# A selective scan beside a decoded FFN: the scan's drive through ScalarE and TensorE transposes, two steps in each turn

## The reference

```python
# FFN of layer 0, h is the normalised x, wg, wu, wd are decoded from control points
out = (silu(h @ wg.T) * (h @ wu.T)) @ wd.T
# scan of layer 1, for each batch: channel d of 512, state n of 16, time l of 512
# delta = softplus(...), u = silu(conv(context @ in_proj))
state[d, n, l] = exp(delta[d, l] * A[d, n]) * state[d, n, l - 1] + delta[d, l] * u[d, l] * B[n, l]
y[d, l]        = sum over n of state[d, n, l] * C[n, l]  + D[d] * u[d, l]
```

## Time and profile before

| what | us |
|---|---|
| median of three runs (1612.72 to 1623.57) | 1617.37 |
| the profiled execution: device time | 1603.47 |
| its span | 1601.7 |
| PE, DVE, ACT, POOL busy in the span | 1322.5, 1092.9, 839.4, 1049.8 |
| stage B, from its first DMA to the last add | 182 to 855 |

### The profile page before, as it was taken

The page is one execution under the profiler, slowest core; times in us unless marked ns, Lnnn a source line. Parts: engine busy times, 40 slices in busy tenths (PEclk is TensorE's granted clock), DMA queues, the critical chain, the costliest instruction groups (busy, mean ns, idle before and its releaser), DMA issues. The chain is left out here.

```text
span 1601.7 us, 24508 instructions
## 1 busy us (share of the span) xinstructions
PE 1322.5 (83%) x5493; PEld 881.7 (55%) x5494; DVE 1092.9 (68%) x1961; ACT 839.4 (52%) x1363; POOL 1049.8 (66%) x656
## 2 busy tenths in 40 slices
PE   7999768987867776675765846999999999999997
PEld 3444323333423332332323435888888988888886
DVE  5777666666867687776777796666656666566554
ACT  6777634446645555564544673454444444454442
...
GB/s 298 119 104 76 185 125 124 137 118 191 173 196 178 221 181 191 179 217 190 179 181 238 267 35 103 202 204 193 200 188 191 207 196 200 198 200 199 197 142 121
DMA packets 108664, 282.09 MB, mean 176 GB/s; under 512 B 17329, under 2 KB 23138, under 8 KB 97474
## 3 DMA queue, kind: packets, MB, share of 16 engines
...
## 5 line engine op out<-in xcount | busy, mean ns | idle before, releaser
L857 PE MATMUL bank<-B_Wd,B_inter 128*128 128x512 f32 x512 | 282.7, 704 | 134.0 <-DVE X L1045 119.6
L1166 POOL TENSOR_TENSOR B_E<-B_dtu,B_BC 128x512 f32<-128x512 f32 (+3 forms) x121 | 312.4, 2734 | 15.7 <-DMA B_BC<-bc_d 15.7
L946 ACT ACTIVATE bank<-B_dtv,negA 128x512 f32<-128x512 f32 x256 | 175.2, 690 | 231.6 <-DVE B_E L1059 120.7
L2087 POOL DMA_INDIRECT out_x<-D_y,D_rows x144 | 234.1, 1626 | 82.6 <-issue 50.2
L1172 POOL TENSOR_TENSOR B_E<-B_E,B_BC 128x1536 f32<-128x1536 f32 x64 | 240.2, 3753 | 71.7 <-DVE B_E L1059 68.0
L857 PEld LDWEIGHTS bank<-B_Wd,B_inter 128*128 128x128 f32 x512 | 110.0, 225 | 306.5 <-issue 291.0
L1059 DVE TENSOR_TENSOR_SCAN B_E<-bank,B_E 128x512 f32<-128x512 f32 x192 | 227.5, 1210 | 32.0 <-ACT bank L946 17.6
L2052 POOL DMA_INDIRECT D_rows<-rows_d,D_source x144 | 153.7, 1067 | 125.8 <-DMA out_x<-D_y,D_rows 63.0
L1913 ACT ACTIVATE D_xT_hi<-bank 128x512 fp32r<-128x512 f32 x147 | 88.0, 599 | 230.1 <-PE bank L1822 229.6
L1833 PE MATMUL bank<-W_gu_hi,D_xT_hi 128*128 x584 | 200.8, 344 | 8.4 <-ACT D_xT_hi L1913 8.4
L1834 PE MATMUL bank<-W_gu_lo,D_xT_hi 128*128 x584 | 198.1, 339 | 0.0
...
...
## 6 DMA issues: line engine op xcount, KB each, us to landing
...
B_BC<-bc_d SPq DMA_DIRECT2D x128, 256.0 KB, 6.2
...
```

Source lines behind the costliest of these rows:

```text
L857: mm = pe.matmul(ps[:, :], chunk(4 * quarter + i)[:, t * P:(t + 1) * P], Wd[:, (4 * quarter + i) % NCH, :], start=i == 0, stop=i == 3)
L946: act.activation(dA[m % 2][:, :], dtv[:, c, :], ACT.Exp, scale=negA[:, c, n:n + 1]).then_inc(dA_done, 1)
L1166: g.tensor_tensor(E[:, s % NR, c:end, :], dtu[:, at:at + end - c, :], spread(BC[op % NBC][:, :], end - c), ALU.mult).then_inc(dbu_done, 1)
L2087: g.indirect_dma_start(a["out"], bass.IndirectOffsetOnAxis(ap=rows[i][:, ROW - 1:ROW].bitcast(U32), axis=0), ysb[:, i, :], None, compute_o ...
```

## The change

- The drive no longer comes from GpSimd. Stage A transposes `dtu` (four chunks of four 128x128 turns in each batch, TensorE into banks, ScalarE out of them) and stores it with time on partitions (`dtuT_d`); the rows B are transposed too and stay in SBUF (`BT`). In stage B ScalarE's `scale(s, t)` multiplies 128 time steps by B as a per-partition scalar into one of six buffers `scaled`, and TensorE's `drive(s, c)` turns four 128x128 blocks into one of two banks, where the scan reads them.
- The decays are written into `E`, in which the scan then writes its state in place; they wait for the gather of four steps before.
- GpSimd weighs all four chunks in two halves, `weigh_last` is gone, and only rows C are loaded (ring of two).
- The order of every engine in stage B is new: TensorE takes a `drive` and one part of the turn by turns, `down` is cut in halves and alternates between two banks, ScalarE prepares a whole step ahead of its scan in two parts, VectorE runs the eight scans of a turn with the rest between them. Turns have two steps (turns 7 and 15 one), and two steps remain after turn 31, beside the last four `down`. The statistics for later norms move from turns 1 and 2 to turns 9 and 10, one unit moves from turn 4 to turn 5, and some buffers are shared.

```diff
-TURN_UNITS += [[("gate_up", 5)] + [("down", k) for k in range(12, NCH)], [("gate_up", 6)], [("gate_up", 7)]]
+TURN_UNITS += [[("gate_up", 5)] + [("down", k) for k in range(12, NCH - 1)], [("gate_up", 6), ("down", NCH - 1)], [("gate_up", 7)]]
...
 ROW = D + NE + 1
...
+            def turn_dtu(b, c, ps):
+                for t in range(LT):
+                    mm = pe.transpose(ps[:, t * P:(t + 1) * P], dtu[:, c, t * P:(t + 1) * P], ident[:, :])
+                mm.then_inc(xT_ps, 1)
...
+                    if b:
+                        if e == 0:
+                            pe.wait_ge(dtu_done, b)
+                        if e == 2:
+                            pe.wait_ge(xT_sb, b * 9 - 3)
+                        else:
+                            pe.wait_ge(x1_done, b * 4 - 4 + (1, 2, 0, 4)[e])
+                        turn_dtu(b - 1, e, bank[DTU_BANK[e]])
+                        if e == 1:
+                            pe.wait_ge(x1_done, b * 4 - 1)
+                            turn_inputs(b - 1, bank[BT_BANK])
...
+            pe.wait_ge(c_sb, NB * 3)
+            pe.wait_ge(dtu_done, NB)
+            for c in range(KC):
+                turn_dtu(NB - 1, c, bank[2 + c])
+                if c == 1:
...
+
+            def dtu_turned(b, c, ps):
+                act.wait_ge(xT_ps, b * 9 + 5 + c + (c > 1))
+                act.activation(dtuT[:, :, c * P:(c + 1) * P], ps[:, :].rearrange("p (t d) -> p t d", t=LT), ACT.Copy).then_inc(xT_sb, 1)
...
+                    if b:
+                        dtu_turned(b - 1, e, bank[DTU_BANK[e]])
...
+                    for c in range(2):
+                        dtu_turned(b, c, bank[2 + c])
                     root_kept()
+                    for c in range(2, KC):
+                        dtu_turned(b, c, bank[2 + c])
...
-                    g.wait_ge(stored, b * 64)
+                    g.wait_ge(xT_ps, b * 9)
...
+            def load_row(s):
+                if s >= NC:
+                    sp.wait_ge(prod_done, 2 * (s - NC) + 2)
+                sp.dma_start(C_row[s % NC][:, :], bc_d[s // NS, NS + s % NS:NS + s % NS + 1, :].broadcast_to([P, L])).then_inc(ld_c[s % NC], 16)
...
+            for s in range(NC, STEPS):
                 b, n = s // NS, s % NS
-                if drives and n == NS - 1 and b < NB - 1:
...
+                load_row(s)
+                if b < NB - 1:
+                    if n == 8:
+                        load_dtu(b + 1, 0)
...
-            def down(n, ps):
+            def down(n, ps, half):
...
+                if half == 0:
...
+                    pe.wait_ge(used, chunk_job(2 * quarter + 1, 1) + 1)
+                    if n >= 2:
                         pe.wait_ge(add_done, n - 1)
...
+                    if n % 2 and n < 4 * (TURNS // 2 - 1):
+                        pe.wait_ge(f_lo, min(2 * quarter + 2 + t // 2 + 2, TURNS))
...
+                for i in range(2 * half, 2 * half + 2):
                     mm = pe.matmul(ps[:, :], chunk(4 * quarter + i)[:, t * P:(t + 1) * P], Wd[:, (4 * quarter + i) % NCH, :], start=i == 0, stop=i == 3)
-                mm.then_inc(y_ps, 1)
+                if half:
+                    mm.then_inc(y_ps, 1)
...
+            def drive(s, c):
+                m = KC * s + c
+                if m >= 2:
+                    pe.wait_ge(s_done, m - 1)
+                for t in range(LT):
+                    if c == 0:
+                        pe.wait_ge(scaled_done, LT * s + t + 1)
+                    mm = pe.transpose(drive_bank[m % 2][:, t * P:(t + 1) * P], scaled[:, (LT * s + t) % NSC, c * P:(c + 1) * P], ident[:, :])
+                mm.then_inc(drive_ps, 1)
...
-                gate_up(jj, 0)
-                gate_up(jj, 1)
-                sums = sums_at(jj)
-                if jj % NG == NG - 1 and jj < TURNS - 1:
-                    for t in range(LT):
-                        turn(LT * (jj // NG + 1) + t)
-                    pe.wait_ge(hT_done, LT * (jj // NG + 2))
-                    down(sums[0], Y_bank)
-                    features(jj + 1)
-                    down(sums[1], Y_bank)
-                else:
-                    if jj < TURNS - 1:
-                        features(jj + 1)
-                    for m in turn_units(jj):
-                        weights(m)
-                    for n in sums:
-                        down(n, Y_bank)
-            for t in range(LT):
-                down(2 * TURNS - 4 + t, T_bank[t % 2])
+                sums, units, steps = sums_at(jj), turn_units(jj), slots(jj)
+                PARTS = 8 + len(units)
+                for i, (s, c) in enumerate(steps):
+                    drive(s, c)
+                    for k in range(PARTS):
+                        if k * len(steps) // PARTS != i:
+                            continue
+                        if k < 2:
+                            gate_up(jj, k)
+                        if k == 2 and not last_of_batch(jj) and jj < TURNS - 1:
+                            features(jj + 1)
+                        if k == 2 and last_of_batch(jj):
+                            for t in range(2):
+                                turn(LT * (jj // NG + 1) + t)
+                        if k == 3 and last_of_batch(jj):
+                            for t in range(2, 4):
+                                turn(LT * (jj // NG + 1) + t)
+                        if k in (5, 7) and k // 2 - 2 < len(units):
+                            weights(units[k // 2 - 2])
+                        if k >= 4 and k < 8 and sums:
+                            if last_of_batch(jj) and k == 4:
+                                pe.wait_ge(hT_done, LT * (jj // NG + 2))
+                                features(jj + 1)
+                            down(sums[(k - 4) // 2], sum_bank(sums[(k - 4) // 2]), k % 2)
+                        if k >= 8 and k - 6 < len(units):
+                            weights(units[k - 6])
+            for i, (s, c) in enumerate(slots(TURNS)):
+                drive(s, c)
+                if i < LT:
+                    for half in range(2):
...
-                m, b, n = KC * s + c, s // NS, s % NS
-                if m >= 2:
-                    act.wait_ge(s_done, m - 1)
-                if s and c == (NW + 2) % KC:
-                    act.wait_ge(last_done, s)
+                b, n = s // NS, s % NS
+                if s >= NR:
+                    act.wait_ge(acc_done[s % 2], 16 * ((s - NR) // 2 + 1))
                 if n == 0:
                     act.wait_ge(ld_dtv[c], 16 * (b + 1))
-                act.activation(dA[m % 2][:, :], dtv[:, c, :], ACT.Exp, scale=negA[:, c, n:n + 1]).then_inc(dA_done, 1)
+                act.activation(E[:, s % NR, c, :], dtv[:, c, :], ACT.Exp, scale=negA[:, c, n:n + 1]).then_inc(dA_done, 1)
+                if n == NS - 1 and b < NB - 1:
+                    load_dtv(b + 1, c)
...
+            def scale(s, t):
+                b, n, m = s // NS, s % NS, LT * s + t
+                if m >= NSC:
+                    act.wait_ge(drive_ps, KC * ((m - NSC) // LT) + KC)
+                if n == 0 and b == 0:
+                    act.wait_ge(ld_dtu[t % 2], 32)
+                elif n == 0:
+                    act.wait_ge(ld_dtu[t % 2], 16 * (2 * b + t // 2 + 1))
+                act.activation(scaled[:, m % NSC, :], dtuT[:, (LT * b + t) % NDU, :], ACT.Copy, scale=BT[:, b, t, n:n + 1]).then_inc(scaled_done, 1)
+
+            def prepare(s, part):
+                if s >= STEPS:
+                    return
+                if part == 0:
+                    scale(s, 0)
+                    decay(s, 0)
+                    scale(s, 1)
+                    decay(s, 1)
+                else:
+                    decay(s, 2)
+                    scale(s, 2)
+                    scale(s, 3)
+                    decay(s, 3)
...
-            decay(0, 0)
-            decay(0, 1)
             feature_hi(0)
+            prepare(0, 0)
+            prepare(0, 1)
...
-                decay(2 * jj, 2)
-                decay(2 * jj, 3)
+                steps = sorted({s for s, c in slots(jj)})
+                units = turn_units(jj)
+                turns = last_of_batch(jj)
+                prepare(steps[0] + 1, 0)
                 silu(jj, 0)
                 silu(jj, 1)
...
+                if turns:
+                    for t in range(2, 4):
+                        turned(LT * (tb + 1) + t)
+                prepare(steps[0] + 1, 1)
...
+                for i, s in enumerate(steps[1:]):
+                    prepare(s + 1, 0)
...
+                    prepare(s + 1, 1)
...
                 m = KC * s + c
-                v.wait_ge(dbu_done, drives_until(s, c))
                 v.wait_ge(dA_done, m + 1)
-                state = E[:, s % NR, c, :] if c < NW else dA[m % 2][:, :]
-                v.tensor_tensor_scan(state, dA[m % 2][:, :], E[:, s % NR, c, :], 0.0, ALU.mult, ALU.add).then_inc(s_done, 1)
-
-            def weigh_last(s):
-                op = weigh_op(s)
```

(48 more changed lines are left out.)

295 lines of the change are left out of this document (126 added, 169 removed).

## The result

The changed kernel takes 1783.46 us (median of four runs, 1781.42 to 1789.56), the kernel before 1617.46 in runs beside it: 1.103 times as long, 95% interval 1.0984 to 1.1076, so 166 us more. The profiled execution of the changed kernel spans 1779.6 us against 1601.7, 178 more. The sum of the prediction had 106.5.

A forecast was written before the change was run, and what follows sets the result against it. GpSimd was taken to bound the kernel from turn 8 on, afterwards a chain of waits through TensorE and ScalarE. 12.5 + 1 + 34 + 10 + 13 + 18 + 18 = 106.5 on 1603.5 gave 1710, raised to 1715 us; range 1600 to 1790.

The forecast's parts named there:

- ScalarE's late answer: Plain turn: drive B0 waits for scalings behind `feature_hi`, table load and a decay; answer 3.8 us, TensorE stands some 3.3.
- its own chain: Whole kernel: the prediction's main case, turns set by waits between engines, range 1655 to 1775 us, chance 0.48.
- signs named beforehand: GpSimd near 70% after turn 8, TensorE standing about 3 us before drive B0, turns 19 to 20, stage B some 765.
- The plain turn: Stage B, two steps without units: walk of 18.8 us plus 0.7 for the clock, 19.5 us against 18.3 before.
- Turns 0 to 7: Decoding turns of stage B: 242.5 us, +34 on 208.2; bounds +15 at full clock, +67 at low.
- my three: Decoding turns: waits of `mult`, `unit_lo` and `blend` behind scans A3, B1 and B2, 2 us each.
- The last turn of each batch: Stage B: one-step turns 7 and 15 at 19.5 us each, the boundary turn of batch 2 at 23.
- Stage A: +12.5 us, bounds 5 and 16: transposes 7.5 over three batches, and the store 5 us later at the end.
- The end of stage B: Two remaining steps and last downs: 36 us after 18.6 before, +18, bounds 10 and 22; batch 3 another +18.
- The next engine takes over: Rival: plain turn is TensorE's 15.2 us without a wait, ScalarE's answer hidden; 1571 us, chance 0.20.
- Half hidden: Rival's variant: ScalarE's answer partly hidden, turn 17.3 us, decoding at +15, about 1640 us, chance 0.10.
- The clock falls: Rival: decoding's clock level 0.72 comes to all of stage B, turn 22 us, about 1800 us, chance 0.12.

The follow-up runs named there:

- runs 1 to 3: Changed kernel with scalings 2 and 3 before the decays: 1722.6 us; with Copy for Silu, no table loads: 1704.0; with added products filling TensorE's stand: 1746.7.
- runs 6 and 7: Features' low parts written after the fourth scan, not the fifth: on the changed kernel 1767.8 us; on that with scalings before decays 1701.6.
- run 5: Changed kernel with one step in each of the first eight turns, threes in seven later turns, drives ahead of the second unit in one-step turns: 1708.4 us.
- run 4: Kernel before with GpSimd's drives cut to 32 of 512 columns and the scan reading `dtu`, factor B left out: 1558.9 us, ratio 0.968.
- run 10: Changed kernel with scalings before decays, steps laid where cheap, TensorE's next features behind drive A3, `feature_hi` behind B's scalings: 1630.3 us against 1642.2 without the features' move.
- run 12: run 10 with first-half scalings before decays, batch-end scalings before the last transposes' copies, a step moved from turn 0 to 28: 1617.4 us, ratio 1.0007 to before.
- run 11: Changed kernel with scalings before decays, low parts after the fourth scan, steps laid where cheap, each drive transpose made twice: 1702.6 us against 1642.2 with single transposes.
- run 3: Changed kernel with four extra product pairs on TensorE between drives A3 and B0 of plain turns after turn 7: 1746.7 us.

## Why the prediction was right, and where it was off

**The sign and its reason.** The forecast said slower by ScalarE's late answer in front of drive B0, not by any engine's work. The timeline shows the wait at the place named, with `feature_hi`, the load and a decay before the scalings, and runs 1 to 3 show that it costs what it seems to: with a decay moved out of it the kernel gets 61 us shorter (54 by the ratios). The number is another matter: the forecast was 98 us more, measured are 166. That lies outside the 1655 to 1775 that the prediction gave its own chain; 1783 is in the stated range only by the room that was left beyond that. Of the signs named beforehand, the stand, its releaser and the turn of 19 to 20 us came; stage B lasted 831 us and not 765, and GpSimd was busy 51 to 53% and not near 70% after turn 8, since its half weighings took 2.38 us and its issues 0.87 where 2.62 and 1.19 had been put in.

**The plain turn.** Said 19.5, measured 19.3 (mean of turns 8 to 14) and 19.8 (16 to 22), settling at 20.4. Its terms, from 701.53: `features` done at 5.2 (said 6.1); from there to the first half down 4.3 (3.8 and a drive of 0.5, so 4.3); four downs' halves and three drives 8.2 (8.4); clock 2.7 (0.7). The last is the term that was mis-sized. The walk also has a slip: the parts of ScalarE's answer, 0.6 + 1.28 + 0.61 + 0.61 + 0.69 and 0.3, are 4.1 and not 3.5, so with the 0.3 for the queue's start it should have said 4.4 and a turn of 20.1. From `features` to the end of the second scaling were 4.0 (706.72 to 710.71), and only two transposes were left of drive B0, so that 4.3 came out right by chance. For the clock I had taken the bound of 1.7 from a down that came back to speed within itself; here 3.62, 1.06 and 2.48 us stand where 1.88, 0.60 and 1.88 would. The other terms made up for half of it; that the mean is 19.3 and 19.8 and not 20.4 comes from turns that kept their clock. The fullest engine's sum, TensorE's 15.2, was 14.3.

**Turns 0 to 7**, said +34, measured +73.5, is the term that made most of the miss. My turns of 32, 32, 38, 38, 38, 24, 21 and 19.5 were 21.1, 36.0, 41.4, 48.3, 43.3, 37.0, 21.7 and 33.0. Of the 39 us, 19 lie in turns 2 to 4, 13 in turn 5, 13.5 in turn 7, and -7 in turns 0 and 1. In turns 2 to 5 the step that failed is the price of the waits. The walk missed one: the odd sum's down waits for `feature_lo`, which I had not among my three; runs 6 and 7 put it at 15 us. The rest is what run 5 shows: a step among units costs 17.7 us, because a drive behind a unit holds a scan, the scan a blend, the blend the next unit, and the clock falls to 0.71. I had counted each wait as a scan and an operation, 2 us; on TensorE they were that (2.06 and 2.69), but VectorE and ScalarE stood 7 to 11 us at a time, and nothing in the sum was for that. Nor do the sums hold by themselves: 27 and 39 put at 32 go with 35 and 47 put at 40, not 38, and all low is 78 + 141 + 64.5 = 283.5, not 275. The bound of +67 should have been +75, and the measured +73.5 all but reached it.

**The last turn of each batch.** Said 19.5, 19.5 and 23; measured 33.0, 28.5 and 30.7. That is 13.5, 9 and 7.7 us and explains nearly all that batches 1 and 2 missed. I gave these turns the price of their work; in the kernel before they take 35.8, 33.8 and 34.9, and followed by a short one of 6.6, so one look at the marks of before would have shown that they are chains of their own.

**Stage A**: said 12.5, measured 15.8. GpSimd's last `dtu` product began at 183.88 and not at 173.14, which is 10.7 for the transposes of three batches (said 7.5); from its start to the store of `dtu` were 4.6 us (173.14 to 177.69) and to that of `dtuT` 9.6 (to 193.47), which is the 5 at the end, as said. In the runs with the same stage A the first DMA of stage B came between 192.3 and 198.2, so this term is known to some 3 us.

**The end of stage B**: turns 24 to 30 took 130.0 against 112.0 and the rest 73.4 against 45.5; said +36 in all, measured 45.9. The first 18 came in seven turns where eight had been said; what remained grew by 27.9 where 18 had been said, and no run took it apart.

**The rivals.** *The next engine takes over* (0.20) was a real possibility that the order kept out: run 4 shows that a freed GpSimd leaves 53 us to win in the old order, where the DMA share is then 0.97, and run 10's plain turn of 15.5 is near the 15.2 of that rival. Its 1571 no version reached: the best, run 12, is level with the kernel before. Half hidden (17.3 a turn, some 1640) is where run 10 is in time, by a shorter turn and longer decoding. *The clock falls* (0.12) is partly what happened, in size: 0.88, 0.83 and 0.89 after turn 8, but 2.7 us a turn. Added transposes don't lower it: in run 11 twice as many raised the granted clock of turns 16 to 23 from 0.94 to 0.98, while filling the stand with products in run 3 raised it over turns 8 to 23 from 0.85 to 0.96. The Trainium skill (TensorE: Matmul & The Clock Gate, "Part 4: PE-mode transpose") says that transposes don't count as the engine being busy for the gate; no run here has transposes without products between them, so the rule is neither shown nor excluded, and it didn't decide.

**What stays open.** Why the same stand of 2.54 us cost clock 14 times out of 17 and not always, and what lengthened the end behind turn 30. The 5 us in stages C and D are no finding: in twelve profiled executions with the same code there, the changed kernel's and those of its versions, these stages took 743.2 to 758.7 us.
